# Attention step of a fused attention and feed-forward layer: another order of TensorE's matmuls over the PSUM banks

## The reference

```python
x = x + attention(layernorm(x), Wq, Wkv, Wo)      # x: 4 x 512 x 1024
x = x + (layernorm(x) @ dequantized(qweight).T + bias)

q = (h @ Wq).reshape(b, s, 32, 32)                # 32 heads of 32
k, v = split(h @ Wkv)                             # one key head, one value head, for all 32
scores = q @ k.T * 32 ** -0.5 + slope[head] * (key - query)
scores = where(key <= query, scores, -inf)        # causal
out = (softmax(scores) @ v).reshape(b, s, 1024) @ Wo
```

## Time and profile before

| | |
|---|---|
| median of three runs | 813.16 us |
| the profiled execution | 815.87 us, its span 814.1 us |
| PE busy | 802.0 us (99%) |
| DVE busy | 594.1 us (73%) |
| ACT busy | 370.3 us (45%) |
| POOL busy | 428.5 us (53%) |
| scores, L877 (PE) | 512 matmuls, 151.3 us |
| units, L906 (PE) | 352 matmuls, 129.7 us |
| values, L917 (PE) | 1024 records, 83.0 us |
| maxima, L1496 (DVE) | 512, 219.5 us |
| exponentials, L1198 (ACT) | 352, 178.1 us |

### The profile page before, as it was taken

One profiled execution on the slowest core, in us unless ns is written; L12 is line 12 of the kernel. 1 busy time (PEld: TensorE's weight loads), 2 busy tenths in 40 slices (PEclk: granted clock), 3 DMA queues, 4 the chain that ended last, 5 costly groups with the idle time before them and its releaser, 6 DMA issues.

```text
span 814.1 us, 13658 instructions
## 1 busy us (share of the span) xinstructions
PE 802.0 (99%) x4624; PEld 583.3 (72%) x4624; DVE 594.1 (73%) x1594; ACT 370.3 (45%) x728; POOL 428.5 (53%) x311
## 2 busy tenths in 40 slices
PE   7999999999999999999999999999999999999998
PEld 5788888888656555656565655688887788888886
DVE  5885575657878889988888896364737768684878
ACT  2757355321566776667666665221401231041322
POOL 1000000000489988898898988431746387464465
PEclk9999999999999999999999999999999999999999
DMA  9867676566555555565467635452063613510112
GB/s 345 308 212 256 221 243 233 180 191 188 160 136 143 134 147 152 152 156 134 127 171 167 163 101 186 152 168 90 1 234 130 227 44 98 187 39 1 39 66 104
DMA packets 71534, 125.85 MB, mean 155 GB/s; under 512 B 7476, under 2 KB 16980, under 8 KB 71384
## 3 DMA queue, kind: packets, MB, share of 16 engines
q1 hardware_dynamic: 70592, 123.53, 49.5%
q10 hardware_dynamic: 872, 1.45, 0.5%
HBM read 85.61 MB, written 38.94 MB: 153 GB/s over the span
## 4 chain that ended last, share of the span: by engine, by line
PE 88%; DMA 4%; DVE 4%; issue 2%; POOL 1%; ACT 1%; ACTq 0%; SPq 0%; DVEq 0%; POOLq 0%
PE p_s L877 12%; PE p_st L906 10%; PE p_o L917 10%; PE p_o L816 7%; PE p_s L816 6%; PE p_o L930 5%; PE p_s L985 5%; PE p_s L986 5%; PE p_s L987 5%; PE p_o L818 3%; DMA inv_b<-inv_d 3%; PE p_s L818 3%; PE p_st L985 2%; PE p_st L986 2%; PE p_st L987 2%; PE p_s L1009 2%
## 5 line engine op out<-in xcount | busy, mean ns | idle before, releaser
L1496 DVE CUSTOM_DVE_ANT_0 spill<-p_s,mask 128x128 bf16<-128x128 f32 (+3 forms) x512 | 219.5, 483 | 41.6 <-PE p_s L877 41.5
L1198 ACT ACTIVATE pt<-p_st 128x512 f32<-128x512 f32 (+1 forms) x352 | 178.1, 562 | 101.8 <-PE p_st L906 101.6
L645 POOL TENSOR_SCALAR_AFFINE_SELECT pt<-pt 128x512 f32<-128x512 f32 x128 | 88.5, 704 | 234.9 <-ACT pt L1198 234.9
L877 PE MATMUL p_s<-kst,xt 98*128 98x128 f32 (+3 forms) x512 | 151.3, 343 | 0.9 <-DVE mx L1496 0.7
L906 PE MATMUL p_st<-xt,kst 100*128 100x512 f32 (+1 forms) x352 | 129.7, 388 | 0.3 <-ACT pt L1198 0.2
L877 PEld LDWEIGHTS p_s<-kst,xt 98*128 98x128 f32 x512 | 91.7, 189 | 52.7 <-DVE mx L1496 42.3
L652 POOL TENSOR_TENSOR pt<-pt 128x1536 f32<-128x1536 f32 x32 | 112.2, 3507 | 2.7
L917 PE MATMUL p_o<-pt,vst 128*32 128x512 f32 (+3 forms) x1024 | 83.0, 441 | 0.0
L658 POOL TENSOR_TENSOR pt<-pt 128x1024 f32<-128x1024 f32 x32 | 76.7, 2396 | 0.0
L906 PEld LDWEIGHTS p_st<-xt,kst 100*128 100x128 f32 x352 | 64.8, 191 | 13.7 <-issue 5.5
L816 PE MATMUL p_o<-xt,wqh 128*128 128x512 f32 x136 | 53.1, 400 | 0.8 <-DVE xt L1667 0.8
(11 more groups left out here) (212 smaller groups left out, 1621.6 us busy)
## 6 DMA issues: line engine op xcount, KB each, us to landing
xt<-qh_d SPq DMA_DIRECT2D x64, 256.0 KB
qh_d<-qh SPq DMA_DIRECT2D x32, 256.0 KB, 2.1
ql_d<-ql SPq DMA_DIRECT2D x32, 256.0 KB, 2.2
xt<-ql_d SPq DMA_DIRECT2D x32, 256.0 KB
o_d<-o_st SPq DMA_DIRECT2D x32, 256.0 KB, 2.1
ob<-o_d SPq DMA_DIRECT2D x32, 256.0 KB, 4.7
xs<-in_x_t_dram SPq DMA_DIRECT2D x28, 256.0 KB, 5.2
xin<-in_x_dram SPq DMA_DIRECT2D x14, 512.0 KB, 6.0
```

Source lines behind the costliest of these rows:

```text
L645: pool.affine_select(out=own, in_=own, compare_op=ALU.is_ge, fill=0.0, base=0, pattern=[[0, 4], [1, P]], channel_multiplier=-1).then_inc(c ...
L877: pe.matmul(scores_of(n), qst[s % 4][0:R_MAX, j, qb * P:(qb + 1) * P], kst[0:R_MAX, b * S:b * S + keys], start=True, stop=True).then_inc(s ...
L1198: act.activation(pt[s % 2][:, j:j + heads, PT_AT[kb]:PT_AT[kb] + KB_LEN[kb]], p_st[:, place(k) % 3, 0:heads * KB_LEN[kb]].rearrange("p (j ...
L1496: dve.tensor_tensor_reduce(spill[:, SPILL_AT[qb]:SPILL_AT[qb] + keys], scores_of(n), mask[:, S - keys:S], 1.0, LOWEST, ALU.add, ALU.max, m ...
```

## The change

TensorE's string of a step is written anew, with letters for the scores: "A" is a head's short score (now block 1 first and block 0 after it), "B" block 2, "C" block 3. `written(n)` gives the count of scores that TensorE has issued once block n is there, for the waits on `s_done` and on the queries (for the first eight heads, n under 32, which are issued during the last projection, the old order stays). T's place in the ring goes from 2 to 4; `max_high` on ScalarE, which stands by `TURN_AT`, moves with it, and `max_low` on VectorE from after a step's fourth maximum to after its fifth. The three groups now stand behind the short scores of the second, third and fourth head.

```diff
-TURN_AT = 2
+TURN_AT = 4
...
+        def written(n):
+
+            return n + 1 if n < 32 or n % 4 > 1 else n + 2 if n % 4 == 0 else n
...
         def turned_max(s):
-            return p_st[:, (TURN_AT if s > 0 else 2) % 3, 0:P]
+            return p_st[:, (TURN_AT if s > 1 else 2) % 3, 0:P]
...
-                if n % 16 == 0:
+                if written(n) % 16 == 1:
                     pe.wait_ge(q_in[s % 4], 64 * (s // 4) + 64)
-                if qb != 1:
+
+                if qb != (1 if n < 32 else 0):
                     at_least(pe, max_done, n - qb - 4 + BANK_LAST[qb] + 1)
...
                 before = RING * s + at - 3
-                if before % RING == TURN_AT:
+                if (s, at) == (0, 2):
+                    pe.wait_ge(ml_done, 2)
+                elif before % RING == TURN_AT:
...
-            ORDER = "xuxuxTGxuxuxuxuGuxuxxuuxGxu"
+
+            ORDER = "uAuuBuCTAGuBuuCAGuuBCuAGBuC"
+            BLOCKS = {"A": (1, 0), "B": (2,), "C": (3,)}
...
-                n, units, groups = 4 * (4 * s + AHEAD), 0, 0
+                n, units, groups, heads = 4 * (4 * s + AHEAD), 0, 0, 0
...
-                    elif what == "x":
-                        for _ in range(2 if n % 4 == 0 else 1):
+                    elif what in BLOCKS:
+                        for qb in BLOCKS[what]:
                             if n < 4 * HEADS_ALL:
-                                score(n)
-                            n += 1
+                                score(n + 4 * heads + qb)
+                        heads += what == "C"
...
-                    dve.wait_ge(s_done, n + 2 if qb == 0 else n + 1)
+
+                    dve.wait_ge(s_done, max(written(n), written(n + 1)) if qb == 0 else written(n))
...
-                    if i == 3 and 0 < s < STEPS - 1:
+                    if i == 4 and 0 < s < STEPS - 1:
                         max_low(s + 1)
```

## The result

The kernel after takes 814.67 us (median of 20 runs, 812.96 to 815.95) against 813.44 us before (20 runs, 812.34 to 814.95), a ratio of 1.0017 with a 95% interval of 1.0010 to 1.0024. It is slower by 1.2 us; I had forecast 810.0. The stated range, 807.6 to 815.0, holds the measured time near its upper end, where I had put rivals 1 and 2; neither of them came about. The profiled execution took 814.11 us, its span is 812.4.

What follows compares the result with a forecast made beforehand. TensorE was taken to pace the steps, 9.40 us each. A change of -0.14 over 29 steps makes -4.1; with +1.6, -0.3 and -0.4 that is -3.2, from 813.16 to 810.0 us; range 807.6 to 815.0.

Steps and rivals of the forecast that it cites:

- rivals 1 and 2: Rival 1, chance 0.20; and, second, longer waits for exponentials at each step's start, 816.7 us, chance 0.15.
- The two stops for VectorE: Short score and C waiting for maxima in each step: both stops go, 0.12 us less per step.
- the ring of three banks: At a step's start, units and T wait for exponentials three places before: 0.13 us more per step.
- T's 0.03: At T in the ring of three banks: T starts 0.03 us late, waiting for an exponential.
- What stands ahead of a group: A block of 128 columns now precedes each group, three times a step: saves 0.15 us per step.
- Rival 1: At each group: the way in costs 0.10 us also behind a short score; 814.4 us, chance 0.20.
- Steps 9, 17 and 25: Where ScalarE copies row sums, T now waits for a later exponential: 3 x 0.55, 1.6 us more.
- Steps 30 and 31: Steps without scores: longer wait ahead of the group, units behind groups free; saves 0.3 us.
- Step 0 and the way into step 1: VectorE is the limit; TensorE does more before step 1's first group: saves 0.4 us, bounds 0.9 saved, 0.5 lost.
- rival 5: In attention steps, new stops close together lower TensorE's clock: 8 us if every fourth step, 818 us; chance 0.02.

Runs made afterwards that it cites:

- e5: e1 with block 0 of each head scored ahead of block 1, so 256 columns stand right ahead of each group; 814.0 us, ratio 1.0013.
- e3: e1 with ScalarE's copies of the row sums moved behind the exponential of u6 instead of u0; 808.99 us, ratio 0.9952.
- e2: The kernel before with `q_low` one maximum later in step 0, so that GpSimd's addition begins first; 817.83 us, ratio 1.0055.
- e7: The kernel before with `q_low` of step 0 moved to the earlier place it has in e1; 814.51 us, ratio 1.0015.
- e1: The kernel after with `q_low` five maxima sooner in step 0; 809.64 us, ratio 0.9956.
- e4: The kernel after with step 0 in the old order and the new order from step 1 on; 809.8 us, ratio 0.9957.
- e8: e4 together with the edit of e3 to the row sums' copies; 807.74 us, ratio 0.9932.

## Why the prediction was wrong

The forecast was 3.2 us faster; it came out 1.2 slower. By its own terms:

- *The two stops for VectorE, -0.12, and the ring of three banks, +0.13.* Both held. The stops' durations are those above, and e5 shows the sum of the two at zero. Whether T's 0.03 is ScalarE's or VectorE's can't be told: of the two it waits for, an exponential and a maximum, the ends lie 0.03 us apart in the step at 307.6 (307.45 and 307.48).
- *What stands ahead of a group, -0.15.* Held: 0.27 us from the pair to the group, and 4.4 us in e5. Rival 1, the way in costs 0.10 behind a short score as well, named 814.4 us and comes nearest to the measured time, by chance: its mechanism would have left the steps at 9.38, and they are 9.23. The 0.27 fits the drain at a change of tiling mode that the Trainium skill states ("TensorEngine Tiling (Array Packing)", Key Properties).
- *Steps 9, 17 and 25, +1.6.* The wait is there, 3 x 0.55 us over the new order's other steps, and the edit of e3 takes it away. But against the kernel before the same three stretches cost less: up to the T of steps 9 and 25 it already took 9.65 and 9.70 us, 0.6 us together over the others, and so did e2 and e7. That is not the row sums (a score of step 8 and one of step 24 start late there, the latter behind a wait of 0.52 us for VectorE), and the new order is free of it (9.23 in e3). I had looked at the mean alone. With it the three stretches cost +1.0.
- *Steps 30 and 31, -0.3.* From the last T to the start of the twenty-fifth tile of the output projection, 33.51 us became 32.58; 0.47 of that is T's later place (two units), 0.46 is gain.
- ***Step 0 and the way into step 1*, -0.4, bounds -0.9 and +0.5. This is the step that failed.** From the first T to the third, 20.84 us became 24.41; less T's later place that is +3.1 against the profile before, and up to 1.5 more, some +4.6, against a usual run of it, which has the full clock there. I wrote that step 1's first group "has to wait for VectorE about as long as before". What VectorE did there was not as before: the stop of 2.78 us is the maxima behind a `q_low` that GpSimd's addition holds up. The bound of +0.5 was missing an instruction that can grow to four times its length. In e1, without it, the same stretch is 19.74 us: less T's later place 1.6 us under the profile before. Of that, up to 1.5 us are the low clock of that one execution, so the place itself was worth about 0.1 and not the 0.4 that I counted.

The five-microsecond difference from e1 has two parts. `q_low` is 2.27 us longer, and the clock is at 1.2 GHz for 6.8 us where e1 has none, some 3.4 us if TensorE had worked through all of it, which it did not. From first to second T that is 14.44 against 10.48, from second to third 9.97 against 9.26: 4.0 + 0.7 = 4.7 of the 5.0 us. e2 shows the same pair in the old order. How much each costs by itself no run tells: where `q_low` came second (after, e2), the clock fell while TensorE stood still for it. Something of the clock's price can be read from the runs of the kernel after: the seven with a mean of 0.998 have a median of 814.3 us, the eleven with 0.996 one of 815.1, so that 0.002 of clock, about another 3.4 us at 1.2 GHz, goes with 0.8 us. The two groups overlap.

I could have seen it. The row of `q_low` in the trace before, 0.04 us ahead of a GpSimd instruction that then took 0.46 us more than its kind, stood in the very stretch whose window I quoted, and I took the window's sums for its content. The rule quoted above was there to be weighed against that row, and I weighed others. The low clock of that window I took for the kernel's own, though the execution stood 2.7 us above the median.

The whole account, from the first T to the start of the twenty-fifth tile: 317.25 us in the trace before, 317.24 after, 312.59 in e1. With the 1.5 us of low clock taken from before, after loses 1.5 us and e1 gains 3.2, where the measured medians say a loss of 1.2 and a gain of 3.6 (interval 2.7 to 4.6). So the 2.4 us by which the profile before stands above its median are that stretch and a longer stop in the output projection (1.27 us at 636.76, 0.19 to 0.27 us at the same place in the other traces looked at: after, e1, e2, e3 and e7). The longer steps 27 and 28, some 0.27 us together (after, e1, e3, e4, e5, e8), were in no term of mine, and I did not follow them up.

## What to carry to other kernels

Where a reordering moves work by tenths of a microsecond, look for the pairs on VectorE and GpSimd that are that close now, and ask what happens when the other one begins first: of the two, the later is held for the rest of the earlier, and it matters which of them TensorE waits for. A term bounded by "about as long as before" is not bounded until every instruction in its stretch has been read with its neighbours. If such an instruction stands in the way, give it room on both sides instead of winning by 0.04 us: e1's place leaves 1.1 us to the addition but only 0.12 to the masking ahead of it, and in the old order the same place lost to that masking (e7). And before a profile's stretch of low clock is put into a sum, compare that execution's mean clock with those of the other runs.

## What the runs showed of the hardware that I had not expected

- The contention is lopsided: `q_low` grew from 0.69 to 2.96 and 3.79 us when it came second (after, e2), GpSimd's addition from 3.44 to 3.51 (e1, e2) to 3.96 or 3.97 us when it did (before, e4). A masking of 0.64 us does the same to it in small (1.11 us, e7). The later one waits out the earlier; the earlier is not slowed.
- Stops of 0.57 and 0.43 us on the way into step 1 left the clock at 2.4 GHz in e1, while in the profile before, with stops of 0.23, 0.06 and 0.51 us in that stretch, it fell to 1.2 for 3.4 us. The kernel alone does not decide it: 30 of 34 other runs of the kernel before have a mean clock of 0.999 or more. What separates the cases no run here shows. Behind the long stops of 2.78 us (after) and 3.62 us (e2) the mean clock was 0.998 or less in all 25 runs of these two kernels.
- In attention 29 steps with three small stops each, 0.13 us together, left the clock at 1.00; rival 5 did not come about, and the low clock came from one long stop instead.
- What a way into a group costs depends on how short the matmul ahead of it is: 0.10 us behind a unit of 384 columns, 0.04 us behind a 128-column score (the pair takes 0.27 there and 0.23 in the stream).
